# Copying both parts of a rotated chunk in one transfer, and another order of work between two sequences

## The reference

```python
q = rope((X @ Wq) as 16 heads of 64); k = rope((X @ Wk) as 8 heads); v = X @ Wv   # a k/v head serves 2 q heads
att = 50 * tanh((q @ k.T) / 16 / 50); att = causal softmax(att)
x = layernorm(X + (att @ v) @ Wo)
q8, s = per-token int8 quantisation of x                 # round(x / (absmax / 127))
y = float16((q8 @ weight.T) * s * w_scale + bias)
out = layernorm(x + y)
```

## Time and profile before

| | us |
|---|---|
| median of 3 runs | 1449.77 (1449.18 to 1451.56) |
| the profiled execution's own time | 1441.84 |
| its span, first to last instruction | 1440.1 |
| PE busy in the span | 1305.8 (91%) |
| DVE / ACT / POOL busy | 1037.5 / 897.0 / 374.3 |

### The profile page before, as it was taken

How to read it: one execution, slowest core, us unless ns; L and a number is a source line. 1 busy time by engine, 2 the same in 40 slices (tenths; PEclk the granted TensorE clock), 3 DMA queues, 4 the chain that set the end, 5 groups by cost and what they waited for, 6 DMA issues and landing times.

```text
span 1440.1 us, 17493 instructions
## 1 busy us (share of the span) xinstructions
PE 1305.8 (91%) x5824; PEld 949.7 (66%) x5840; DVE 1037.5 (72%) x1303; ACT 897.0 (62%) x1016; POOL 374.3 (26%) x450
## 2 busy tenths in 40 slices
PE   6569999899897999999897999989989799999895
PEld 5457777676565777766665677767666477777563
DVE  4369888884567888887455888888636688888565
ACT  4157777772356777866244787776425677779454
POOL 1331111111462111111265111111127311112266
PEclk9879999999898999999999999999999899999897
DMA  8756444466523344538641445453853154343551
GB/s 291 254 181 196 112 109 118 137 190 189 156 70 96 104 117 132 143 103 236 178 108 59 97 127 137 102 157 92 264 139 104 57 143 105 105 105 100 150 134 51
DMA packets 120773, 196.22 MB, mean 136 GB/s; under 512 B 26470, under 2 KB 68972, under 8 KB 116844
## 3 DMA queue, kind: packets, MB, share of 16 engines
q1 hardware_dynamic: 114924, 185.15, 46.6%
q10 hardware_dynamic: 5760, 9.97, 2.0%
HBM read 89.39 MB, written 38.54 MB: 89 GB/s over the span
## 4 chain that ended last, share of the span: by engine, by line
PE 67%; SPq 7%; DVE 6%; POOL 6%; DMA 6%; issue 4%; ACT 3%; ACTq 0%; POOLq 0%; DVEq 0%
PE ps L740 23%; PE ps L660 15%; PE ps L714 15%; PE ps L682 6%; PE ps L782 6%; SPq L434 4%; POOL y_lo L1337 2%; DMA rows<-r_scratch 1%; DVE stats L1212 1%; DMA y_scratch<-sums 1%; DVE prob_hi L1132 1%; POOL f L1355 1%; POOL probs L1357 1%; POOL rstd L1346 1%; DMA div<-y_scratch 1%
## 5 line engine op out<-in xcount | busy, mean ns | idle before, releaser
L740 PE MATMUL ps<-prob_hi,v 128*65 128x512 f32 (+3 forms) x1280 | 418.5, 377 | 4.7 <-DVE prob_lo L1136 4.7
L924 ACT ACTIVATE probs<-ps 128x1024 f32<-128x1024 f32 x288 | 293.6, 1019 | 156.0 <-PE ps L714 153.0
L714 PE MATMUL ps<-qk 128*128 128x512 f32 (+1 forms) x1280 | 320.1, 377 | 54.7 <-DMA qk<-work_r 27.6
L1136 DVE TENSOR_TENSOR prob_lo<-probs,prob_hi 128x1024 fp32r<-128x1024 f32 x288 | 360.1, 1250 | 9.9
L1331 POOL TENSOR_SCALAR_AFFINE_SELECT probs<-probs 128x256 f32<-128x256 f32 (+1 forms) x192 | 144.6, 760 | 809.6 <-ACT probs L929 809.6
L929 ACT ACTIVATE probs<-probs 128x1024 f32<-128x1024 f32 x288 | 305.5, 1061 | 8.8
L714 PEld LDWEIGHTS ps<-qk 128*128 128x128 f32 x1280 | 227.7, 191 | 117.5 <-ACT probs L924 29.8
L660 PE MATMUL ps<-xT,w_ring 128*128 128x512 f32 x1152 | 291.9, 397 | 10.4 <-DVE xT L1074 8.3
L1132 DVE CAST prob_hi<-probs 128x1024 fp32r<-128x1024 f32 x288 | 206.4, 717 | 122.4 <-POOL probs L1331 72.4
L660 PEld LDWEIGHTS ps<-xT,w_ring 128*128 128x128 f32 x1152 | 218.5, 192 | 57.6 <-DVE xT L1074 9.6
L740 PE MATMUL ps<-prob_lo,v 128*65 128x512 f32 (+1 forms) x640 | 240.4, 376 | 0.0
(11 more groups left out here) (79 smaller groups left out, 996.2 us busy)
## 6 DMA issues: line engine op xcount, KB each, us to landing
qk<-work_r SPq DMA_DIRECT2D x256, 128.0 KB, 2.3
qk<-work_r SPq DMA_DIRECT2D x488, 64.0 KB, 2.0
y_scratch<-sums SPq DMA_DIRECT2D x128, 130.0 KB
wo<-wo_scratch SPq DMA_DIRECT2D x8, 2048.0 KB, 7.7
y_raw<-y_scratch SPq DMA_DIRECT2D x64, 256.0 KB, 4.3
w_ring<-w_scratch SPq DMA_DIRECT2D x15, 1024.0 KB, 5.9
x_raw<-X_T SPq DMA_DIRECT2D x16, 512.0 KB, 4.9
x_in<-X SPq DMA_DIRECT2D x32, 256.0 KB, 4.3
```

Source lines behind the costliest of these rows:

```text
L714: mm = nc.tensor.matmul(scores[:, g % 2, col:col + REP * w].rearrange("p (h q) -> p h q", h=REP), qk[:, n % 2, i, 2 + part, keys], qk[:, n ...
L740: mm = nc.tensor.matmul(sums_ps[:, :, GQ - w:GQ], v[:, kt, v0:v0 + width], p[:, at, col:col + REP * w].rearrange("p (h q) -> p h q", h=REP ...
L924: nc.scalar.activation(probs[:, prob_place(g), :], scores[:, g % 2, :], ACT.Tanh, scale=SCORE_SCALE / SOFTCAP).then_inc(capped, 1)
L1136: nc.vector.tensor_tensor(prob_lo[:, prob_place(g), :], probs[:, prob_place(g), :], prob_hi[:, hi_place(g), :].bitcast(F32), ALU.subtract) ...
```

## The change

It has four parts.

1. One call of `put` copies both parts, after `rope_low`. k: 4 transfers, each from 32 partitions with 2 x 1024 elements, each row written twice, to 64 partitions. q: 8 transfers from 32 partitions x 2 parts x 512 to 64 partitions. In `qk` the low part now lies ahead of the high one and the rows of a head alternate; k and q are laid out alike. ACT no longer requests the last put of a sequence.
2. PE computes score(0) of the next sequence before the row phase and score(1) after its last `project_out`; ACT caps step 0 within the row phase, step 1 ahead of norm2 of tile 6, step 2 ahead of norm2 of tile 7. The last two tiles of `project_v` use other banks.
3. residual2 of tile 6 goes ahead of the mask of step 0 on POOL, stats2 and the last rescale ahead of the probabilities of step 0 on DVE. invert(0) stands behind the last probabilities (in the last sequence: a step earlier).
4. SP requests in another order: x of the next sequence in steps 12 and 13, y of the first tiles in step 15, the rows for tile t + 4 in iteration t, and w_scale, bias and the ring of weights behind the rows.

```diff
-        def put(eng, m, x, low):
-            eng.wait_ge(rope_lo if low else rope_hi, chunks_upto(m, x))
+        def put(eng, m, x):
+            eng.wait_ge(rope_lo, chunks_upto(m, x))
...
+            parts = work_r[:, place_of(m, x), :, :].bitcast(F32)
...
                     for half in range(2):
-                        src = work_r[64 * half + 32 * i:64 * half + 32 * (i + 1), place_of(m, x), 1 - low, :].bitcast(F32)
-                        for copy in range(2):
-                            r0 = 64 * copy + 32 * half
-                            eng.dma_start(buf[r0:r0 + 32, i, 2 + low, :].bitcast(F32), src
-                                         ).then_inc(k_put[m % 2][i], 16)
+                        src = parts[64 * half + 32 * i:64 * half + 32 * (i + 1)].rearrange("p a t -> p (a t)")
+                        eng.dma_start(buf[64 * half:64 * (half + 1), i, 2:4, :].rearrange("p a t -> p (a t)").bitcast(F32),
+                                      src.unsqueeze(1).broadcast_to([32, 2, 2 * T])).then_inc(k_put[m % 2][i], 16)
...
                         for half in range(2):
-                            src = work_r[32 * h:32 * (h + 1), place_of(m, x), 1 - low, half * HT:(half + 1) * HT].bitcast(F32)
-                            r0 = 64 * low + 32 * half
-                            eng.dma_start(buf[r0:r0 + 32, i, r, cols].bitcast(F32), src
-                                         ).then_inc(q_put[m % 2][x - 1][i], 16)
+                            eng.dma_start(buf[64 * half:64 * (half + 1), i, r, cols].bitcast(F32),
+                                          parts[32 * h:32 * (h + 1), :, half * HT:(half + 1) * HT]
+                                          ).then_inc(q_put[m % 2][x - 1][i], 16)
...
             for x in range(3):
-                put(sp, 0, x, 0)
-                if x == 0:
+                if x == 1:
                     sp.wait_ge(projected, chunks_upto(0, 0))
                     load_wk(1)
-                put(sp, 0, x, 1)
+                put(sp, 0, x)
...
-                        if u == 2 and b + 1 < B and s in (14, 15):
-                            load_x_turned(b + 1, s - 12)
-                            if s == 15:
-                                load_wq(m + 1)
+                        if u == 2 and b + 1 < B and s == 13:
+                            load_x_turned(b + 1, 2)
+                            load_x_turned(b + 1, 3)
+                        if u == 2 and b + 1 < B and s == 15:
+                            load_wq(m + 1)
...
@@ tensor @@
                 if more:
                     project_v(b + 1, 6)
                     project_v(b + 1, 7)
+                    score(b + 1, 0)
...
                 m = UB * b + UB + 1
+                if more:
+                    score(b + 1, 1)
                 turn_q(b, NT - 2)
...
                 if more:
-                    score(b + 1, 0)
                     project(m, 0, 8, 16)
```

More of the change, by code:

```diff
@@ L331, in wait_put @@
             for i in range(2):
[L332 removed]
+                if x == 0:
+                    eng.wait_ge(k_put[m % 2][i], k_puts_upto(m))
+                else:
+                    eng.wait_ge(q_put[m % 2][x - 1][i], q_puts_upto(m))
         def prob_place(g):
@@ L574, in _ @@
                             load_div(b, 0)
-                        if at := chunk_at(b, u, s, turns(u, 5, 10, 14)):
-                            put(sp, *at, 0)
-                        if (at := chunk_at(b, u, s, turns(u, 6, 11, 15))) and at != (UB * b + UB, 2):
-                            put(sp, *at, 1)
+                        if at := chunk_at(b, u, s, turns(u, 6, 11, 15)):
+                            put(sp, *at)
                         if s == turns(u, 0, 0, 12)[2] and m < U:
@@ L618, in _ @@
                     load_x(b, t)
+                load_rows(b, 2)
+                load_rows(b, 3)
                 for t in range(NT):
+                    if t < 2:
+                        store_inverse(b, t + 2)
+                    if t + YRING < NT:
+                        load_y(b, t + YRING)
+                    if t + XRING < NT:
+                        load_x(b, t + XRING)
+                    if t + 4 < NT:
+                        load_rows(b, t + 4)
                     if t == 1 and b + 1 < B:
@@ L715, in score @@
                             scores[:, g % 2, col:col + REP * w].rearrange("p (h q) -> p h q", h=REP),
-                            qk[:, n % 2, i, 2 + part, keys], qk[:, n % 2, i, 0:REP, q0:q0 + w],
+                            qk[:, n % 2, i, 3 - part, keys], qk[:, n % 2, i, 0:REP, q0:q0 + w],
                             start=(part == 0), stop=(part == 1))
@@ L864, in _ @@
                 linear(b, NT - 1)
-                if more:
-                    score(b + 1, 1)
         @block.scalar
@@ L1021, in _ @@
                             split_wo(s)
+                keep_sums(b, NKV - 1, G - 2)
                 if more:
-                    put(act, UB * b + UB, 2, 1)
-                keep_sums(b, NKV - 1, G - 2)
-                keep_sums(b, NKV - 1, G - 1)
-                if more:
+                    keep_sums(b, NKV - 1, G - 1)
                     for t in range(4):
@@ L1029, in _ @@
                 round_y(b, 0)
+                if not more:
+                    keep_sums(b, NKV - 1, G - 1)
                 if more:
@@ L1044, in _ @@
                     norm1(b, t - 1)
+                    if more and t == NT - 1:
+                        cap(b + 1, 0)
                     if t >= 3:
@@ L1054, in _ @@
                 if more:
-                    cap(b + 1, 0)
                     exponent(b + 1, 0)
+                    cap(b + 1, 1)
                 keep_q(b, NT - 1)
+                if more:
+                    exponent(b + 1, 1)
                 norm2(b, NT - 2)
@@ L1060, in _ @@
                 if more:
-                    cap(b + 1, 1)
-                    exponent(b + 1, 1)
+                    cap(b + 1, 2)
+                    exponent(b + 1, 2)
                 norm2(b, NT - 1)
@@ L1261, in _ @@
                             rope_read(*at)
-                        if u == UB - 1 and s == 17:
+                        if (b, u, s) == (B - 1, UB - 1, 16):
                             invert(b, 0)
@@ L1270, in _ @@
                 probs_of(b, NB - 1)
+                if more:
+                    invert(b, 0)
                 invert(b, 1)
@@ L1302, in _ @@
                 rescale(b, NT - 2)
+                stats2(b, NT - 2)
+                rescale(b, NT - 1)
+                shift_by(b, NT - 2, 1, rstd2, shift2)
                 if more:
                     probs_of(b + 1, 0)
-                stats2(b, NT - 2)
-                shift_by(b, NT - 2, 1, rstd2, shift2)
-                rescale(b, NT - 1)
+                stats2(b, NT - 1)
                 if more:
-                    probs_of(b + 1, 1)
-                stats2(b, NT - 1)
+                    round_probs(b + 1, 1)
                 shift_by(b, NT - 1, 1, rstd2, shift2)
+                if more:
+                    low_probs(b + 1, 1)
         @block.gpsimd
```

48 lines of the change are left out of this document (23 added, 25 removed).

## The result

| | before | changed |
|---|---|---|
| median (lowest to highest) of 4 runs, us | 1449.47 (1447.4 to 1451.56) | 1403.68 (1401.43 to 1405.22) |
| the profiled execution, its span | 1441.84, 1440.1 | 1401.43, 1399.7 |
| ratio, 95% interval | | 0.969 (0.9675 to 0.9706) |

The change takes 45.8 us off the median; the two profiled executions differ by 40.4. Forecast were 51 us and 1399, with 1383 to 1422 as the range. One execution in this study, in the last experiment, ran at a reduced clock (1651 us) and is left out of the ratios.

A forecast was written before the change was run, and what follows sets the result against it. PE was taken to bound the kernel, busy 1305.8 of 1440.1 us, losing time to idle and half clock at five places. Terms 5 + 7.5 + 18.6 + 16.5 + 3.5 = 51 us off 1449.8 gave 1399, range 1383 to 1422.

The forecast's parts named there:

- Mid units, puts at 0: Puts in mid-unit: SP saves 5 to 7.5 us a chunk under a PE that is full, so 0 us gained.
- First scores, 5: Start of the kernel: first score 2.5 us earlier and PE's second wait gone, 5 us; bounds 0 and 5.6.
- x of the next sequence, 7.5: Where unit 3 begins: x requested before the put, less idle and half clock, 2.5 us three times, 7.5.
- Seam's start, 0: Start of each seam: score(0) adds about 1.1 us of PE work, counted under the early row phase; 0 here.
- Early row phase, 18.6: Early row phase: PE's wait for tile 3's rows goes, clock recovers, w_scale costs 1.6; 6.2 us three times, 18.6.
- Late row phase, 16.5: End of row phase: caps freed, DVE binds next and starts rope_read earlier; 5.5 us three times, 16.5.
- Last sequence, 3.5: Last sequence: rows and PE's start 1.9 us earlier, second wait loses 1.5; 3.5 us, bounds 0 and 6.5.
- the wait for w_scale: Rival, early row phase: the wait moves to w_scale, all of the 18.6 goes, 1417 us; chance 0.15.
- ACT waits for stores at caps 2 and 3: Rival, end of row phase: ACT is held by store landings, all of the 16.5 goes, 1415 us; chance 0.11.
- the 4 that was set as the sign: Sign of a wrong forecast: caps 2 and 3 each waiting over 4 us for a store.
- k transfers took longer than they should: Rival, mid units: large k transfers exceed their cover and hold DVE, then PE; 1459 us at 23 us; chance 0.05.
- the 19 us of cover: Mid units: time k's 2 MB may take before DVE is held at rope_read, then PE, in 15 units.

The follow-up runs named there:

- e5: Changed kernel with k put in two calls again, high part a step earlier, new layout kept: 1394.44 us, ratio 0.9639 to the kernel before.
- c1: The changed kernel itself, unaltered, run again on another chip as a reference: 1400.66 us, ratio 0.9683 to the kernel before.
- e1: Changed kernel with the old put of the kernel before, everything else as changed: ratio 0.9668 to the kernel before.
- e2: Kernel before with nothing but the new put: ratio 1.0005 to the kernel before.
- e8: Changed kernel with the 2 MB load of Wo's high part requested right behind the w_v loads: ratio 0.9704 to the kernel before.
- e7: Changed kernel with w_scale and bias requested right after the rows of tiles 2 and 3: 1396.93 us, ratio 0.9655 to the kernel before.
- e11: Changed kernel with SP's request order in the row phase as before: ratio 0.9875 to the kernel before.
- e4: Changed kernel with POOL's and DVE's order at the end of the row phase as before: 1418.75 us, ratio 0.9815 to the kernel before.
- e9: Changed kernel with k put in two calls, w_scale and bias early, and Wo's load behind w_v: ratio 0.9626 to the kernel before.
- e10: Changed kernel with k put in two calls and w_scale and bias early, Wo's load as changed: 1390.23 us, ratio 0.9599 to the kernel before.

## Why the prediction was right, and where it was not

- **Mid units, puts at 0.** Right: 58.00 in 58.00 still, and the new put alone changes nothing that can be measured. The price under it was wrong for k: four requests cost SP 7.4 to 7.6 us there, not 4 x 0.63 = 2.5, so SP saves 2.4 us a k chunk and not 7.5. Under a full PE that is worth nothing either way.
- **First scores, 5.** Wrong: 1.6. The step that failed is the transfer time of k. I took 284 GB/s from a window in which a load from HBM (w_ring, requested at 66.11) was under way as well, 7.4 us for 2 MB; k took 14.4 us from the first request, no less than before (13.65), from a start 3 us later. The Trainium skill's fit ("DMA: Bandwidth & Descriptors", "Anatomy of one DMA") would have given an estimate of 6.8 us, further off still; the section gives it for transfers that GpSimd requests, and the puts are requested by SP. The Trainium skill's other section there, "Issuing engines are not separate DMA queues", says that transfers run on the same 16 DMA engines whichever engine requests them. It does not speak of the number of requests; that fewer requests save only the requester's time was my step from it, and the runs agree with that: 14.4 us against 13.65 for the same 2 MB, and 7.63 us of SP against 9.98. Only the second wait went, as worked out. Sending the high part of k early again (e5) gives what was missed.
- **x of the next sequence, 7.5.** Right in kind: ACT does not wait behind the put, 1.61 us of idle were left where 1.5 were forecast, and no half clock. In size 5.5 (3.4, 0.5 and 1.7), and 3.3 in the profile of c1: 2.5 was forecast for each sequence, and the two profiles have -1.0 to 3.4.
- **Seam's start, 0.** Wrong: -9.1, and the largest error. I looked at who issues the puts and when the inverses are stored, and not at w_v, for which PE already waited 1.23 us. The three waits grew by 6.2 us, and half clock comes behind them. PE came earlier by more than the request did, and w_v took longer to land. With the old put the waits are 3.6 (e1), with the new put alone 9.8 (e2). Shorter rows of k (e5, 10.6) and moving Wo (e8, 7.5) do not cure it. The share of the DMA engines does not tell the kernels apart while w_v is in flight: 0.91 to 1.02 before, 0.98 to 1.00 after. What in the new puts makes w_v late, the merged q perhaps, is open: q was not tried alone.
- **Early row phase, 18.6.** Right: 17.8. The wait for rows went, the clock came back to 1.00, tile 2 was held by split_y (0.24), and w_scale cost what was charged: 1.6 forecast, 1.9 shown by the profile of e7. That undoing SP's order costs 27 us in all (e11) is more than this term explains.
- **Late row phase, 16.5.** Right in size, 18.2, and in mechanism: caps free of norm2, the new wait for the store of 2.12 (2.0 forecast), DVE next. The runs divide it, first seam: undoing POOL's and DVE's order takes 5.4 of 5.9, undoing ACT's 2.1. Each is worth more with the other, since cap(2) behind the store of tile 6 is early only where norm2 of tile 6 is (e4's rows).
- **Last sequence, 3.5.** Wrong: 0.2, and 1.8 in the profile of c1. The lead at round_y of tile 0 did grow by 4.3 us, and the rows of tile 2, which I did not follow, took it back.
- **Attention phases beyond the first scores and x.** Not forecast: some 6 us, with those 13.3.

The sum was 51, the profiles give 40.4 and the medians 45.8. The two row-phase terms, 35 of the 51, were worked out from waits and came out close; that the total is so close is in part luck, since 9 us lost at the seam's start and 6 gained in attention were both outside the sum. The prediction's own low and high figures are 1441 and 1365; its high bounds add up to 77, which makes 1372.

Of the rivals: the wait for w_scale cost 5.8 us in three seams, 1 more than was charged, where its case took all of the 18.6. ACT waits for stores at caps 2 and 3 in every seam, 2.1 to 3.2 us each, under the 4 that was set as the sign, and the end gained all the same. k transfers took longer than they should, but 14 us is inside the 19 us of cover, so no unit is longer.

## What to carry to other kernels

Follow the leader's wait through to the next load: a PE that arrives earlier at a stage gains only if that stage's data is requested and landed earlier too. Merging transfers did not make them faster here. It freed the requester by less than the number of requests suggests. A load's wait has two halves, how far ahead of its reader it is requested and how long it takes to land: read both before blaming either. On an in-order queue, put the request that is awaited soonest ahead of bulk loads that are needed later, and on an in-order engine the short statistics ahead of work that waits for a mask. A transfer that can start with half of its data (k's high part) was worth more started early (e5) than made whole (the changed kernel).

## What the runs showed of the hardware

- What a request costs SP depends on what it asks for. Requests of 128 KB took 0.63 us each, 16 of them 5.02 + 4.96 us for the 2 MB of k. Of four requests of 512 KB for the same bytes the first two took 0.68 and 0.59, the third 4.14 and the fourth 2.08, and in the middle of a unit, from 166.20, 0.54, 0.60, 4.12 and 2.03. The window from 68 to 72 us shows the DMA engines at share 1.01 and 229 GB/s. It looks as if SP were held while the first large ones are under way; no run shows why.
- The same 186.7 MB cost the 16 engines 704 us with k in rows of 8 KB written twice by one transfer (694 to 707 in the seven profiles with this put), 686 with the two copies apart, 674 with rows of 4 KB written twice (666 and 667 in e9 and e10), 681 with the old put (share of queue 1 times the span).
- Where unit 3 begins, after 1.61 us of idle PE was at full clock (8 matmuls in 2.10 us); before the change, after 3.26 us of idle, the same 8 took 3.60 us.
